# First attention of a two-layer image tower: the order of four products around a transposition on TensorE, and of a sum and a copy on VectorE

## The reference, cut to what matters

```python
def _L0_attn_ref(x, Wqkv, bqkv, Wout, bout, alphas_raw):
    B, N, DIM = (4, 512, 128)
    H, DH, ORDER, TOPK = (8, 64, 3, 64)
    qkv = x @ Wqkv + bqkv
    q, k, v = split into 8 heads of 64
    scores = jnp.einsum('bhnd,bhmd->bhnm', q, k) * SCALE
    top_val = jax.lax.top_k(scores, TOPK)[0][..., -1:]
    scores = jnp.where(scores < top_val, -jnp.inf, scores)
    attn = jax.nn.softmax(scores, axis=-1)
    v_curr, res = v, 0
    for i in range(ORDER):
        v_curr = attn @ v_curr
        res = res + gelu(alphas_raw[i]) * v_curr
    return res @ Wout + bout
h = h + _L0_attn_ref(_layernorm(h), ...)
```

## Time and profile before

| | us |
|---|---|
| median of 3 runs | 1859.84 (1859.69 to 1862.83) |
| the profiled execution, its own time | 1857.18 |
| its span, first to last instruction | 1855.4 |
| first attention, in the span | about 310 to 862 |

### The profile page before, as it was taken

One profiled execution on the slowest core, in us unless ns is written; L12 is line 12 of the kernel. 1 busy time (PEld: TensorE's weight loads), 2 busy tenths in 40 slices (PEclk: granted clock), 3 DMA queues, 4 the chain that ended last, 5 costly groups with the idle time before them and its releaser, 6 DMA issues. The chain is left out here.

```text
span 1855.4 us, 61849 instructions
## 1 busy us (share of the span) xinstructions
PE 1666.1 (90%) x24177; PEld 1221.2 (66%) x24177; DVE 1088.4 (59%) x3338; ACT 874.1 (47%) x2369; POOL 777.8 (42%) x925
## 2 busy tenths in 40 slices
PE   8999998898999999987899979999999998459997
PEld 3444443676767667664767747787777777448897
DVE  0000015787877777783667654666767677537765
ACT  0000016665555555554444455656666665236653
POOL 0000000777877777772011102345554555514444
PEclk9999988999999999998699989999999999579999
DMA  9877720000000000003000000000000000124422
GB/s 377 334 303 292 312 102 1 3 4 3 3 3 3 3 3 3 3 4 102 1 1 1 1 1 2 3 14 26 20 19 19 19 22 16 47 74 123 125 72 61
DMA packets 47215, 117.17 MB, mean 63 GB/s; under 512 B 10731, under 2 KB 29470, under 8 KB 46972
## 3 DMA queue, kind: packets, MB, share of 16 engines
q1 hardware_dynamic: 39198, 99.25, 14.9%
q0 software_dynamic: 6096, 12.94, 1.9%
q10 hardware_dynamic: 1678, 1.43, 0.2%
HBM read 96.80 MB, written 18.61 MB: 62 GB/s over the span
## 5 line engine op out<-in xcount | busy, mean ns | idle before, releaser
L1358 PE MATMUL ps<-xn,s_a_wqkv 128*128 128x260 f32 x1024 | 296.8, 408 | 29.1 <-ACT qk_a L768 22.6
L170 PE MATMUL ps<-x_chunk,s_w_tok 128*128 128x512 f32 x576 | 250.7, 596 | 6.2 <-DMA x_chunk<-in_x_main 6.2
L1358 PEld LDWEIGHTS ps<-xn,s_a_wqkv 128*128 128x128 f32 x1024 | 171.1, 192 | 82.2 <-ACT qk_a L768 48.0
L170 PEld LDWEIGHTS ps<-x_chunk,s_w_tok 128*128 128x128 f32 x576 | 109.4, 191 | 146.3 <-issue 146.3
L940 ACT ACTIVATE e_a<-e_a 128x585 f32<-128x585 f32 (+1 forms) x128 | 84.9, 663 | 166.1 <-DVE e_a L1248 95.6
L197 DVE SCALAR_TENSOR_TENSOR h<-ps,s_b_tok,s_pos 128x512 f32 (+1 forms) x16 | 11.3, 746 | 248.1 <-PE ps L178 248.1
L1239 DVE TENSOR_REDUCE neg_max_a<-ps 128x8 f32<-128x520 f32 x128 | 89.2, 697 | 104.7 <-PE ps L1336 104.7
L724 POOL TENSOR_TENSOR prob_a<-e_a,inv_sum_a 128x512 f32<-128x512 f32 x64 | 66.9, 1046 | 197.6 <-issue 107.0
L614 POOL MEMSET cls_queries_a<- 128x1040 f32 x2 | 1.9, 966 | 346.2 <-POOLq L221 346.2
L1442 PE MATMUL ps<-s_a_wqkv,xn_pair_a 128*64 128x256 f32 x1024 | 138.4, 389 | 5.2 <-ACT weightsT_m L875 2.8
L1985 POOL DMA_INDIRECT out<-block_out_m,block_m x93 | 93.5, 1005 | 115.4 <-DVE block_out_m L2088 104.5
(11 more groups left out here) (284 smaller groups left out, 4379.6 us busy)
## 6 DMA issues: line engine op xcount, KB each, us to landing
x_chunk<-in_x_main SPq DMA_DIRECT2D x96, 768.0 KB, 8.6
block_m<-pair_rows SPq DMA_DIRECT2D x93, 130.0 KB, 2.1
pair_rows<-pad_rows_m SPq DMA_DIRECT2D x29, 130.0 KB
s_f_all<-in_f_w SPq DMA_DIRECT2D x2, 1024.0 KB
x_ends<-in_x_tail SPq DMA_DIRECT2D x16, 96.0 KB, 10.7
out<-block_out_m,block_m POOLq DMA_INDIRECT x93
s_w_tok<-in_w_tok SPq DMA_DIRECT2D x6, 192.0 KB, 6.7
pair_rows<-rows_m,slot_i_m POOLq DMA_INDIRECT x65, 2.6
```

What stands on the lines that cost most here:

```text
L170: last = nc.tensor.matmul(ps[:, bank, :], w_tok[:, k, :], xb[:, s, k, :], start=(k == 0), stop=False)
L1358: nc.tensor.matmul(ps[:, QK_BANK[i], 0:QUAD], w_qkv[:, c * P:(c + 1) * P], xn[:, t.h * QUAD:(t.h + 1) * QUAD], start=True, stop=True).then ...
```

## The change

In the first attention alone: on TensorE `project_qk` 2 and 3 stand ahead of `transpose_probs` instead of behind it, in every step; on VectorE `probs_out` stands behind the sum and the reciprocal instead of ahead of them. No instruction is added or removed. The second attention (`masked` false) keeps both orders.

```diff
                 order_out(t, 0)
                 order_out(t, 1)
-                probs_out(t)
+                if not masked:
+                    probs_out(t)
                 if t.has(2):
                     upto(dve, kept_done if masked else exp_done, t.s - 1, pairs)
 ...
                     nc.vector.reciprocal(invs, sums).then_inc(inv_done, 1)
+                if masked:
+                    probs_out(t)
 ...
                     transpose_cls(t)
                     project_v(t)
+                    project_qk(t, 2)
+                    project_qk(t, 3)
                     transpose_probs(t)
                 else:
                     last_product(t)
 ...
                     project_dist(t)
                     transpose_probs(t)
-                project_qk(t, 2)
-                project_qk(t, 3)
+                    project_qk(t, 2)
+                    project_qk(t, 3)
                 project_out(t)
```

## The result

The changed kernel takes 1842.26 us (median of 4 runs, 1838.73 to 1842.97); the kernel before, run beside it, 1860.73 us (median of 4, 1859.69 to 1862.83). The ratio is 0.9898, 95% interval 0.9885 to 0.9911: 18.5 us faster. The prediction was 1840.0 us, range 1835 to 1851.

A forecast was written before the change was run, and what follows sets the result against it. The prediction took TensorE to bound the first attention, idling in waits for ScalarE's copies. It summed 31 x 0.34 + 28 x 0.33 = 10.5 + 9.2 = 19.8 us off the median 1859.84, giving 1840.0 us, range 1835 to 1851.

The forecast's parts named there:

- the two waits: First attention, TensorE: class scores wait 32 times for the key copy, 18.2 us; output projection 28 times for a query copy, 6.2.
- 0.34 us an odd step: Keys, TensorE: class scores start at 605.87 instead of 606.21, set by ScalarE's copies; 31 times, bounds nothing and 0.73 us.
- 0.33 an even one: Queries, TensorE: output projection starts earlier because copy 2 follows the value copy; 0.33 us taken, 28 times.
- the shortening that the prediction named and priced as a bound: Even step: if the projection never waits, it takes 1.85 us to the next scores instead of 1.92, saving 0.42.
- Its other bound: Even step: if products are spaced a little wider behind the narrow value products, the saving is 0.25 us.
- 0.2 to 0.4 us to remain: Sign in the profile after: the class scores' wait falls from 0.57 us to about this, 18.2 us to about 10.
- The cover: Odd step: VectorE's late copy of transposed probabilities ends at 606.51, TensorE's next products start at 606.97, leaving 0.46 us.
- the 0.14 that was taken over from the other direction: VectorE's sum was taken to follow GpSimd's multiplication by 0.14 us, as GpSimd follows VectorE's reciprocal.
- the rival "more": First attention: fill steps move up too, 2 us, and the projection never waits; gain 25 us, time 1835, chance 0.07.
- the two halves fit together: With the transpositions later, an unmoved VectorE copy would hold the sum and reciprocal back to about 606.6.
- Code supply: TensorE stops without a semaphore, left as they are; as a bound take back 0.3 us a quad, 10 us; half-gain rival, 0.11.
- a change of TensorE's clock behind the stage: Rival "nothing remains": 40 us more of the following stage at half clock costs 20 us, time 1860, chance 0.07.

The follow-up runs named there:

- experiment 5: Changed kernel, but class scores of even steps start after three of four key copies and wait for the fourth just ahead of its matmuls; ratio to kernel before 0.9891.
- session A: One group of runs on one chip, with kernel before, changed kernel and each half alone; kernel before 1862.67 us, changed kernel 1842.93 us, ratio 0.9901.
- Experiment 8: Changed kernel plus two unused VectorE reductions of 520 elements between reciprocal and copy in odd steps; 1841.92 us against 1831.52 of the changed kernel, ratio to kernel before 0.9953.
- C: A later group of runs on another chip, repeating the changed kernel beside variants; kernel before 1851.68 us, changed kernel 1831.52 us, ratio 0.9901.

## Why the prediction was right

**TensorE's order.** The mechanism was the one forecast: products 2 and 3 go first, ScalarE's copies move up, and what the two waits cost shrinks in 31 odd and 28 even steps. The size of a step was reckoned a little low, 0.34 us an odd step and 0.33 an even one, 0.67 a quad; measured 0.39 and 0.39, 0.78 at the seams and 0.77 a quad over the 27. (The pair of quads with 15.77 and 15.10 gives 0.67 as well, but that is the luck of the pair.) In the odd step the missing 0.05 is in ScalarE's queue: the reckoning let copy 2 start at the end of the value copy, 0.60 behind its start, and it starts 593.72 - 593.17 = 0.55 behind it. The key copies end at 593.72 + 0.92 = 594.64 and the scores start 0.05 later, as reckoned; experiment 5 moved them by giving up that wait. In the even step the projection starts 586.28 - 584.86 = 1.42 behind product 2, as reckoned (597.00 - 595.58), and takes 1.87 to the next scores instead of 1.92: the shortening that the prediction named and priced as a bound. Its other bound, products spaced wider behind the narrow value products, is real too, 0.98 us to the transpositions instead of 0.88, but it falls beside ScalarE's time.

**One expectation of the profile was read wrongly.** I expected 0.2 to 0.4 us to remain as a listed wait of the class scores. The profile lists none, since it counts from the modelled end of the transpositions; the time is there, 594.69 - 593.96 = 0.73 from start to start where 0.44 is needed in the even step, and only starts show it.

**VectorE's order.** The cover was reckoned at 0.46 us and measured at 0.51; the sum followed GpSimd by 0.04 us and not by the 0.14 that was taken over from the other direction. The copy waits in fill and drain were not foreseen (2.3 us); the prediction had the fill move up by 2 us in the rival "more". That the two halves fit together is true in the mechanism, since without VectorE's half GpSimd's normalisation starts 1.5 us later (1.57 us behind the class scores against some 0.05), but as a time it can't be told: 3.8 us in the 27 quads, of which the ends take 2.4 (session A).

**Code supply.** It was left as it is, and it stayed: in the first attention 19 and 22 stops, 19.5 and 21.7 us, in the two profiles before; 23, 22 and 23 stops, 20.6, 22.2 and 22.4 us, in the three after. The Trainium skill ("Runtime: NRT & Kernel Launch", Instruction fetch mechanics) calls the cost of a block crossing mostly hidden; by count the trace agrees, with about one packet in six followed by a stop, but these stops are of about 1 us each, some 20 us in one stage. Experiment 8 shows that a stop can hide time lost ahead of it. The removal of the two waits was not taken back in that way: 0.78 at the seams is 0.77 in the quads, stops included.

**The sum, and how much of it is luck.** 19.8 us was reckoned. By the measured steps it would have been 31 x 0.39 + 28 x 0.39 = 23.0, 3.2 more, and the seams gave 22.8. The stage gave 22.3 us between the first two profiles, and 20.9 between the means of two profiles before (553.4, 556.7) and three after (531.1, 535.0, 536.2). By time it was 18.5 us in the first comparison, 19.7 in session A and 20.2 in C. So the forecast of the time is close in part by luck: the steps gave 3 us more than reckoned, and 2.6 to 4.3 us are missing between the seams (22.8) and the time (18.5 to 20.2). Of these 0.5 to 1.9 lie in the stage outside the seams; where the rest goes was not found. The stretch to the second attention took 242.7 and 242.3 us before and 241.1 to 242.6 after, so a change of TensorE's clock behind the stage did not take back the gain.

## What to carry to other kernels

Where an engine in order waits for a copy whose input it makes itself, put independent work between the input and the wait, and read from the copying engine's timeline what sets its start next: here ScalarE's value copy, to 0.05 us. Count from start to start over the same short seam in every step, which here gave 0.39 us again and again, while the distance of whole quads scattered by 0.2 us around it and whole runs by 5 us or more. Don't take one pair that fits the forecast. Price a moved instruction by its cover, and look at fill and drain on their own, where the steady state's cover is missing.

## What the runs showed of the hardware

- The second attention, same code, took 533 to 538 us in two sessions (chips) and 545 to 549 in a third, with 10 or 11 stops of 0.2 to 0.4 us in its scores, each lengthening a group of four steps by 0.8 us.
- In the first attention most waits called issue (16 of 19 before, 18 of 23 after) end 1.15 to 1.6 us behind the end of a 16 KB instruction packet; those in the scores of the second attention don't.
- Such a stop can take in what is lost just ahead of it: 1.02 us became 0.27 when TensorE was held back some 0.7 us 1.9 us earlier, and 8.9 us of delay in 16 quads with stops cost 2.8.
- VectorE's reductions of 0.69 us follow each other faster than they last: two take 442.26 - 441.10 = 1.16 us from start to the start of what follows. The copy behind them came 0.42 (one) and 1.04 us (two) later in the median, less where VectorE had been ahead.
- An empty semaphore instruction on TensorE costs about 0.15 us: the stretch from the first attention to the second grew from some 242 to 260.8 us with 128 of them, which includes a longer stretch of granted clock 0.50.
- An output projection of 1.92 us at full clock took 3.66 in a stretch of granted clock 0.50; one such stretch of 3.4 us inside the stage made its quad some 2 us longer.
